# Silu and Softplus written out with Tanh, Exp and Ln in a Mamba-and-experts kernel on one core

## The reference, cut to what matters

```python
xz = xn @ W_in
xb, z = jnp.split(xz, 2, axis=-1)
xp = jnp.pad(xb, ((0, 0), (1, 1), (0, 0)))
xb = conv_w[:, 0] * xp[:, :-2] + conv_w[:, 1] * xp[:, 1:-1] + conv_w[:, 2] * xp[:, 2:] + conv_b
xb = jax.nn.silu(xb)
dt = jax.nn.softplus(xb @ W_dt + b_dt)
...
A_bar = jnp.exp(dt_t[:, :, None] * A)
h = A_bar * h + (dt_t * x_t)[:, :, None] * B_t[:, None, :]
y_t = jnp.einsum('bdn,bn->bd', h, C_t)
...
y = (y + D_param * xb) * jax.nn.silu(z)
```

## Time and profile before

| | |
|---|---|
| median of 3 runs | 2744.53 us (2736.11 to 2752.65) |
| profiled execution: time, span | 2752.65 us, 2750.8 us |
| instructions in the trace | 28773 |
| GpSimd busy | 2234.3 us, 81% |
| longest group: `drive`, L1175 | 512 of 2658 ns |
| scans, L702 | 512 of 2292 ns |
| decays, L1004 | 1024 of 682 ns |
| Softplus, L895 | 64 of 687 ns |
| Silu, L885 and L921 | 64 of 626 ns and 64 of 595 ns |

### The profile page before, as it was taken

One profiled execution on the slowest core, in us unless ns is written; L12 is line 12 of the kernel. 1 busy time (PEld: TensorE's weight loads), 2 busy tenths in 40 slices (PEclk: granted clock), 3 DMA queues, 4 the chain that ended last, 5 costly groups with the idle time before them and its releaser, 6 DMA issues.

```text
span 2750.8 us, 28773 instructions
## 1 busy us (share of the span) xinstructions
PE 2373.8 (86%) x9004; PEld 1696.4 (62%) x9004; DVE 2319.5 (84%) x2255; ACT 1621.4 (59%) x2892; POOL 2234.3 (81%) x1563
## 2 busy tenths in 40 slices
PE   3544798998989899998989999898989989898899
PEld 1222566676756666675666667666666766666678
DVE  1679898989989898988989899898989989898922
ACT  3465756557475656647576665757666575765311
POOL 1678888888989888888888899898888889887922
PEclk7677899999999899999999999999999999999999
DMA  4789898998989899898989999898999989898921
GB/s 114 201 194 253 200 239 216 241 229 219 253 211 246 219 231 237 217 241 211 240 219 240 237 222 250 205 252 220 252 223 221 247 198 244 216 253 214 242 60 51
DMA packets 338380, 596.80 MB, mean 217 GB/s; under 512 B 49697, under 2 KB 160289, under 8 KB 338225
## 3 DMA queue, kind: packets, MB, share of 16 engines
q0 software_dynamic: 72960, 243.30, 46.3%
q1 hardware_dynamic: 265264, 351.64, 40.5%
HBM read 349.89 MB, written 10.06 MB: 131 GB/s over the span
## 4 chain that ended last, share of the span: by engine, by line
PE 48%; POOL 16%; ACT 10%; DVE 10%; issue 9%; DMA 6%; SPq 0%; POOLq 0%; DVEq 0%; ACTq 0%
PE wbank L498 15%; PE mbank L510 9%; POOL unit L1175 7%; PE wbank L397 6%; DVE hbank L702 5%; DMA gsum<-unit 5%; PE wbank L440 4%; PE wbank L526 3%; PE wbank L385 3%; POOL act L1142 2%; POOL gsum L1187 2%; PE wbank L460 2%; DVE unit L716 2%; PE wbank L523 2%; ACT z L823 2%
## 5 line engine op out<-in xcount | busy, mean ns | idle before, releaser
L1175 POOL TENSOR_TENSOR unit<-dtx,b_bc 128x1024 f32<-128x1024 f32 x512 | 1355.3, 2658 | 5.5 <-DMA b_bc<-bc_scratch 3.1
L702 DVE TENSOR_TENSOR_SCAN hbank<-hbank,unit 128x1024 f32<-128x1024 f32 x512 | 1173.5, 2292 | 150.4 <-ACT hbank L1004 126.1
L1004 ACT ACTIVATE hbank<-dt,a_neg 128x512 f32<-128x512 f32 x1024 | 669.2, 682 | 279.8 <-DVE unit L716 246.2
L510 PE MATMUL mbank<-down_t,act 128*128 128x256 f32 x2048 | 526.4, 397 | 77.8 <-POOL act L1142 61.1
L716 DVE TENSOR_TENSOR unit<-hbank,c_bc 128x1024 f32<-128x1024 f32 x448 | 546.5, 1220 | 26.6 <-DVE hbank L702 1.0
L1142 POOL TENSOR_TENSOR act<-act,w_all 128x512 f32<-128x512 f32 x256 | 366.1, 1430 | 211.7 <-DVE act L680 196.4
L1187 POOL DMA_DIRECT2D gsum<-unit x448 | 451.5, 1008 | 100.3 <-DMA gsum<-unit 54.6
L498 PE MATMUL wbank<-h_t,up_t 128*128 128x256 f32 x2048 | 497.5, 387 | 22.8 <-DVE act L673 22.8
L510 PEld LDWEIGHTS mbank<-down_t,act 128*128 128x128 f32 x2048 | 399.7, 199 | 173.3 <-POOL act L1142 83.8
L498 PE MATMUL wbank<-h_t,gate_t 128*128 128x256 f32 x2048 | 487.9, 381 | 12.1 <-ACT gz L921 12.1
L498 PEld LDWEIGHTS wbank<-h_t,up_t 128*128 128x128 f32 x2048 | 394.4, 194 | 114.6 <-DVE act L673 35.2
(11 more groups left out here) (113 smaller groups left out, 2287.4 us busy)
## 6 DMA issues: line engine op xcount, KB each, us to landing
gsum<-unit POOLq DMA_DIRECT2D x448, 512.0 KB, 7.5
c_bc<-bc_scratch SPq DMA_DIRECT2D x464, 256.0 KB, 5.7
b_bc<-bc_scratch SPq DMA_DIRECT2D x448, 256.0 KB, 6.3
w_all<-w_scratch SPq DMA_DIRECT2D x256, 256.0 KB, 4.8
ht<-in_L_attn_x_dram SPq DMA_DIRECT2D x16, 512.0 KB, 5.2
w_out<-in_L_attn_W_out_dram SPq DMA_DIRECT2D x16, 512.0 KB, 5.6
ht<-in_L_attn_x_dram POOLq DMA_DIRECT2D x16, 512.0 KB, 8.8
out_dram<-xt SPq DMA_DIRECT2D x16, 512.0 KB, 3.3
```

Of the source, the lines that this page charges most:

```text
L510: m = eng.matmul(mbank[:, u * H:(u + 1) * H], act[:, (n - 1) % MOE_RING, j, u * P:(u + 1) * P], down_t[:, e, :], start=(e == 0 and u == 0) ...
L702: eng.tensor_tensor_scan(h, h, unit[:, g % RING, :, :].rearrange("p a t -> p (a t)"), 0.0, ALU.mult, ALU.add).then_inc(scanned, 1)
L1004: eng.activation(hbank[g % HB][:, a, :], dt[:, 2 * q + a, :], ACT.Exp, scale=a_neg[:, 2 * q + a, n:n + 1]).then_inc(decayed, 1)
L1175: eng.tensor_tensor(unit[:, g % RING, :, :], dtx[:, 2 * q:2 * q + 2, :], b_bc[:, s:s + 1, :].to_broadcast([P, 2, T]), ALU.mult).then_inc(d ...
```

## The change

Silu and Softplus are no longer asked of ScalarE by name. Silu(x) becomes x/2 * (1 + tanh(x/2)): ScalarE writes Tanh and VectorE does the rest in one scalar_tensor_tensor. For xb the half is folded into conv_w and conv_b, and Tanh is written back into the tile's work bank. The halves for the gates are folded into `diag_d` and into the new `half_ident`, with which y is now summed. Softplus(x) becomes relu(x) + ln(1 + exp(-|x|)): four ACTIVATEs and a tensor_tensor on VectorE. The banks of conv, dt and gate tiles are all freed by VectorE's last operation. The tasks of `silu_inputs` and `gates` handle one tile after the other with two or three steps each.

```diff
@@ xb_ready
-            need.wait_ge(silu_act, DK * (row + 1))
+            t = work.at["conv", row, DK - 1]
+            need.wait_ge(t.free, t.after)
...
@@ PE: mix
-                        m = eng.matmul(t.bank[:, :], ident[:, :], gsum[:, (2 * p + k) % SUMS, a, :], start=False,
+                        m = eng.matmul(t.bank[:, :], half_ident[:, :], gsum[:, (2 * p + k) % SUMS, a, :], start=False,
...
@@ VectorE: silu_inputs, step_sizes, gates
-                    need.wait_ge(conv_v, n)
+                    need.wait_ge(conv_v, 2 * n - 1)
                     eng.scalar_tensor_tensor(out=cv[:, 0:T - 1], in0=t.bank[:, 1:T], scalar=conv_w[:, q, 2:3],
-                                             in1=cv[:, 0:T - 1], op0=ALU.mult, op1=ALU.add).then_inc(t.free, 1)
-                    yield
-                for _ in range(4):
+                                             in1=cv[:, 0:T - 1], op0=ALU.mult, op1=ALU.add).then_inc(conv_v, 1)
+                    yield
+                    yield
+                    need.wait_ge(silu_act, n)
+                    if row and not pair:
+                        y = work.at["y", row - 1, q]
+                        need.wait_ge(y.full, y.after)
+                    eng.scalar_tensor_tensor(out=xb[:, xb_at(row, q), :], in0=t.bank[:, :], scalar=1.0, in1=cv, op0=ALU.add,
+                                             op1=ALU.mult).then_inc(t.free, 1)
+                    yield
+
+            def step_sizes(row, q):
+                for m_ in (2 * q, 2 * q + 1):
+                    t = work.at["dt", row, m_]
+                    yield
+                    need.wait_ge(soft_act, 4 * (DK * row + m_ + 1))
+                    eng.tensor_tensor(dt[:, m_, :], dt[:, m_, :], t.bank[:, :], ALU.add).then_inc(t.free, 1)
+                    yield
+                    yield
+
+            def gates(row):
+                for q in range(DK):
+                    t = work.at["gate", row, q]
+                    need.wait_ge(gate_act, DK * row + q + 1)
+                    eng.scalar_tensor_tensor(out=gz[:, q, :], in0=gz[:, q, :], scalar=1.0, in1=t.bank[:, :],
+                                             op0=ALU.add, op1=ALU.mult).then_inc(t.free, 1)
+                    yield
                     yield
...
@@ VectorE: mix
-                    gate = work.at["gate", row, q]
-                    need.wait_ge(gate.free, gate.after)
...
@@ VectorE: at the start
+            eng.tensor_scalar(conv_w[:, :, :], conv_w[:, :, :], 0.5, None, ALU.mult).then_inc(scaled_w, 1)
+            eng.tensor_scalar(conv_b[:, :], conv_b[:, :], 0.5, None, ALU.mult).then_inc(scaled_w, 1)
...
-                eng.tensor_scalar(diag_d[:, m_, :], ident[:, :], d_par[:, m_:m_ + 1], None,
+                eng.tensor_scalar(diag_d[:, m_, :], ident[:, :], d_par[:, m_:m_ + 1], 0.5, ALU.mult,
                                   ALU.mult).then_inc(scaled_w, 1)
+            eng.tensor_scalar(half_ident[:, :], ident[:, :], 0.5, None, ALU.mult).then_inc(scaled_w, 1)
...
@@ ScalarE: silu_inputs, step_sizes, gates
                     if n > 2:
-                        need.wait_ge(silu_act, n - 2)
+                        before = work.at["conv", *divmod(n - 3, DK)]
+                        need.wait_ge(before.free, before.after)
...
-                yield
-                yield
-                for q in (2 * pair, 2 * pair + 1):
-                    t = work.at["conv", row, q]
-                    need.wait_ge(t.free, t.after)
...
-                    eng.activation(xb[:, xb_at(row, q), :], conv[:, q % 2, :], ACT.Silu).then_inc(silu_act, 1)
-                yield
-                yield
+                    yield
+                    need.wait_ge(conv_v, 2 * n)
+                    eng.activation(t.bank[:, :], cv, ACT.Tanh).then_inc(silu_act, 1)
+                    yield
...
-                    eng.activation(dt[:, m_, :], t.bank[:, :], ACT.Softplus, bias=b_dt[:, m_:m_ + 1]).then_inc(t.free, 1)
+                    x = t.bank[:, :]
+                    eng.activation(dt[:, m_, :], x, ACT.Relu, bias=b_dt[:, m_:m_ + 1]).then_inc(soft_act, 1)
+                    eng.activation(x, x, ACT.Abs, bias=b_dt[:, m_:m_ + 1]).then_inc(soft_act, 1)
+                    need.wait_ge(soft_act, at + 2)
+                    eng.activation(x, x, ACT.Exp, scale=-1.0).then_inc(soft_act, 1)
+                    need.wait_ge(soft_act, at + 3)
+                    eng.activation(x, x, ACT.Ln, bias=1.0).then_inc(soft_act, 1)
...
-                for pair in range(2):
-                    yield
-                    for q in (2 * pair, 2 * pair + 1):
...
-                        eng.activation(gz[:, q, :], t.bank[:, :], ACT.Silu).then_inc(t.free, 1)
-                    for _ in range(4):
-                        yield
+                for q in range(DK):
...
+                    eng.activation(gz[:, q, :], t.bank[:, :], ACT.Tanh, scale=0.5).then_inc(gate_act, 1)
+                    yield
+                    yield
```

More of the change, by code:

```diff
@@ L133, in build @@
         ident = sb("ident", [P, P])
+        half_ident = sb("half_ident", [P, P])
         conv_w = sb("conv_w", [P, DK, 3])
@@ L223, in build @@
             sem(n) for n in ("norm_a", "norm_p", "normed", "conv_act", "conv_v", "silu_act"))
-        dtx_made, dt_cut = sem("dtx_made"), sem("dt_cut")
-        bc_out, w_stored = sem("bc_out"), sem("w_stored")
+        soft_act, dtx_made, dt_cut = sem("soft_act"), sem("dtx_made"), sem("dt_cut")
+        gate_act, bc_made, bc_out, w_made, w_stored = (
+            sem(n) for n in ("gate_act", "bc_made", "bc_out", "w_made", "w_stored"))
         b_in, c_in = [sem(f"b{k}_in") for k in range(B_RING)], [sem(f"c{k}_in") for k in range(C_RING)]
@@ L423, in gates @@
                     m.then_inc(t.full, 1)
-                    if q % 2:
-                        yield
-                        yield
-                        yield
+                    yield
                     yield
@@ L544, in _ @@
             need.wait_ge(weights_in, 16 * N_LOADS)
-            need.wait_ge(scaled_w, 6)
+            need.wait_ge(scaled_w, 9)
             stage_of = {"turn_in": turn_in, "silu_first": lambda r: silu_inputs(r, 0),
@@ L774, in _ @@
             stage_of = {"silu_first": lambda r: silu_inputs(r, 0),
-                        "silu_last": lambda r: silu_inputs(r, 1),
+                        "silu_last": lambda r: silu_inputs(r, 1), "gates": gates,
+                        "step_sizes0": lambda r: step_sizes(r, 0), "step_sizes1": lambda r: step_sizes(r, 1),
                         "mix0": lambda r: mix(r, 0), "mix1": lambda r: mix(r, 1),
@@ L876, in silu_inputs @@
                     yield
-                yield
-                yield
-                for q in (2 * pair, 2 * pair + 1):
-                    t = work.at["conv", row, q]
-                    need.wait_ge(t.free, t.after)
-                    if row and not pair:
-                        y = work.at["y", row - 1, q]
-                        need.wait_ge(y.full, y.after)
-                    eng.activation(xb[:, xb_at(row, q), :], conv[:, q % 2, :], ACT.Silu).then_inc(silu_act, 1)
-                yield
-                yield
+                    yield
+                    need.wait_ge(conv_v, 2 * n)
+                    eng.activation(t.bank[:, :], cv, ACT.Tanh).then_inc(silu_act, 1)
+                    yield
             def step_sizes(row, q):
                 for m_ in (2 * q, 2 * q + 1):
-                    t = work.at["dt", row, m_]
+                    t, at = work.at["dt", row, m_], 4 * (DK * row + m_)
                     need.wait_ge(t.full, t.after)
@@ L912, in gates @@
             def gates(row):
-                for pair in range(2):
-                    yield
-                    for q in (2 * pair, 2 * pair + 1):
[L916 to L920, removed]
-                        eng.activation(gz[:, q, :], t.bank[:, :], ACT.Silu).then_inc(t.free, 1)
-                    for _ in range(4):
-                        yield
+                for q in range(DK):
+                    t = work.at["gate", row, q]
+                    need.wait_ge(t.full, t.after)
+                    if row:
+                        p = work.at["proj", row - 1, 1]
+                        need.wait_ge(p.full, p.after)
+                    eng.activation(gz[:, q, :], t.bank[:, :], ACT.Tanh, scale=0.5).then_inc(gate_act, 1)
+                    yield
+                    yield
             def project(row):
```

## The result

The changed kernel takes 2782.5 us (2777.73 to 2789.72, 4 runs) against 2740.53 us (4 runs): ratio 1.0144, 95% interval 1.0115 to 1.0173. Slower was right, its size was not: +90 us forecast, +42 measured.

What follows compares the result with a forecast made beforehand. VectorE was taken to set the pace where nobody delays it. 16 x (3.3 - 1.7) for step_sizes1 and gates, 15 x (2.2 + 1.8) for step_sizes0 and conv, and 5 gave +90.6 on 2744.5: 2835 us, range 2745 to 2895.

Steps and rivals of the forecast that it cites:

- Sign: Whole kernel: the change makes it slower, given a chance of 0.82.
- loads: ScalarE's table loads: of 16 per batch row 8 go (10.3 us) and 8 stay, four of them at Ln.
- chain: Step sizes: Relu, Abs, Exp, load and Ln take 3.85 us from data to result, 3.16 more than Softplus.
- start: First batch row: nothing to hide behind, one exposed Softplus chain and some hand-overs cost 5 us once.
- step_sizes1: Second Softplus pair of a row: longer chains delay the scans, +3.3 us per row, bounds 1.2 and 6.3.
- step_sizes0: First Softplus pair, for the next row: VectorE full, nothing absorbed, +2.2 us per row, bounds 1.2 and 6.3.
- Gates: Gates' Silu: 2.4 us of added VectorE work less 4.1 of waits that go, -1.7 us per row.
- Conv: Conv tiles' Silu: added VectorE work and a Tanh wait, less idle time behind loads, +1.8 us per row.
- (a): Rival: load traffic idles VectorE and the Ln chains hide, so faster, 2690 us; chance 0.12.
- (b): Rival: PE waits for work banks now freed by VectorE, 2946 us, or 2890 at half of it; chance 0.11.
- (c): Rival: chains hide and only added VectorE work counts, 1.9 us per row plus 5, 2780 us; chance 0.09.
- (d): Rival: Exp and Ln share a table set, so step_sizes1's load back leaves the path, 2814 us; chance 0.06.

Runs made afterwards that it cites:

- soft_last: The kernel before with Softplus written out only for the second pair of a row (step_sizes1); median 2757.6 us, 0.49% slower.
- pe_twice_last: The kernel before with PE's product for the first dt tile of step_sizes1 made twice; 3.3 us more in units 0 to 3.
- soft_no_loads: Kernel before with only Softplus written out, but Tanh in place of Ln, so no table loads at the step sizes; 2750.0 us.
- adds_only: The kernel before, Softplus kept, with one tensor_tensor per dt tile added on VectorE, which also frees the bank; ratio 1.0024.
- soft_first: The kernel before with Softplus written out only for the first pair (step_sizes0); 0.48% slower.
- gates_only: The kernel before with only the gates' Silu written out as Tanh and VectorE operations; 2726.7 us, ratio 0.9945.
- silu_no_adds: The kernel before with both Silus replaced by a bare Tanh, without VectorE's last operation (results differ); 0.6% gained.
- conv_only: The kernel before with only the conv tiles' Silu written out; 0.84% slower.
- softplus_only: The kernel before with only Softplus written out, four ACTIVATEs and an add on VectorE; 2777.7 us, ratio 1.0137.

## Why the prediction was right and wrong

**Sign, loads, chain, start: right.** 8 loads per row stay, at Ln; the chain is 3.75 us; VectorE's row is 150.3. The start cost 6.7 us (first scan at 89.4 and 96.1) for 5.

**step_sizes1, the term that failed: +3.3 us per row forecast, about +0.3 measured by the stages** (+2.0 in units 0 to 3, -1.7 in units 4 to 10). By whole times soft_last, which has this part alone, is 0.49% or 13 us slower, 0.8 us per row, so the term was at least four times too large. Two steps of it were wrong. First, it took the data's arrival from one row. Windows around the start of that row, before and after (columns as in the earlier trace rows):

```profile
1184.00:1188.00 4.00, 2.17 (x11) 1.56 (x9) 3.90 (x4) 1.82 (x3) 3.73 (x3) 1.00 1.03 287
1188.00:1192.00 4.00, 3.21 (x6) 2.15 (x7) 3.90 (x4) 2.58 (x3) 3.94 (x3) 0.57 1.10 239
1192.00:1196.00 4.00, 4.00 (x14) 2.35 (x13) 3.90 (x4) 1.14 (x2) 3.43 (x3) 1.00 1.05 276
```

```profile
1198.00:1202.00 4.00, 2.89 (x14) 2.23 (x13) 3.90 (x4) 1.82 (x3) 3.67 (x3) 1.00 1.06 276
1202.00:1206.00 4.00, 4.00 (x12) 2.12 (x12) 3.90 (x3) 1.30 (x2) 3.25 (x2) 1.00 1.09 258
```

From 1188 to 1192 PE was granted 0.57 of its clock, part of the time 1.2 instead of 2.4 GHz, after a window in which it was busy 2.17 of 4 us. The rows of GpSimd and PE there, then PE's at the same place of an undisturbed row of the same trace (scan of unit 0 at 1509.45), then PE's in the changed kernel:

```profile
1184.27 0.87 POOL L1187 DMA_DIRECT2D gsum<-unit  x1 [1.36 <-DMA gsum<-unit]
...
1187.20 1.54 POOL L1142 TENSOR_TENSOR act<-act,w_all 128x512 f32<-128x512 f32 x1
...
1188.79 2.07 PE L510 MATMUL mbank<-down_t,act 128*128 128x256 f32 x4 [2.62 <-POOL act L1142]
1190.66 4.14 PE L397 MATMUL wbank<-xb,w_dt 128*128 128x512 f32 x8
```

```profile
1507.66 1.13 PE L510 MATMUL mbank<-down_t,act 128*128 128x256 f32 x4 [1.21 <-POOL act L1142]
1508.63 3.60 PE L397 MATMUL wbank<-xb,w_dt 128*128 128x512 f32 x8
```

```profile
1201.73 1.13 PE L510 MATMUL mbank<-down_t,act 128*128 128x256 f32 x4 [1.11 <-POOL act L1166]
1202.70 3.60 PE L400 MATMUL wbank<-xb,w_dt 128*128 128x512 f32 x8
```

The first w_dt product started 1.5 us after the scan of unit 0 there (1189.16), 0.8 us before it in the undisturbed row and 0.9 before it in the changed kernel (1203.61). Units 0 to 3 of the disturbed row took 21.35 us; of 13 rows of the same trace eight took 18.5 to 19.1 and five 20.8 to 21.5; in the second trace one is above 19.5. All five have a granted clock of 0.50 to 0.52 for 3.4 us from just before the scan of unit 0, and the other eight don't. But the clock is only half of it. GpSimd's `add` had waited 1.36 us for a DMA, its `act` for the experts came late, and PE waited 2.62 us for it instead of 1.21: 1.4 us. At the lower clock the four L510 then took 2.07 instead of 1.13 us and the product 4.14 instead of 3.60: 1.5 us. The late row of the second trace has the wait (2.98 us) and the full clock. I had read a disturbed row as the pattern.

Second, the sum pushed the scans by the chain's length and asked only for idle time in the same units. Medians per unit, us, the kernel before over its eight undisturbed rows, the others over 13:

```
unit              0     1     2     3     4     5     6     7     8
before         4.13  4.13  4.09  6.18  4.74  4.92  4.63  4.52  4.72
changed        4.13  6.11  5.71  4.74  4.51  4.92  3.54  4.51  4.34
pe_twice_last  4.13  6.89  5.04  6.18  4.74  4.92  4.63  4.52  4.72
```

Units 1 and 2 lose 3.6 us, near the 4.0 by which the chain was said to move the scans. What the sum missed is what comes back: 1.4 in unit 3, where waits of VectorE for tanh (0.7) and for decays (0.6) are gone, and 1.7 in units 4 to 8; it had let 0.7 be absorbed. A delay on ScalarE's side comes back later, a delay on PE's side does not. In the kernel before, units 6 and 8 wait for decays that stand in ScalarE's queue behind the projection's result, as here:

```profile
1223.28 0.39 ACT L935 ACTIVATE xt<-wbank 128x256 f32<-128x256 f32 x1 [3.68 <-PE wbank L442]
...
1224.80 2.30 DVE L702 TENSOR_TENSOR_SCAN hbank<-hbank,unit 128x1024 f32<-128x1024 f32 x1 [1.01 <-ACT hbank L1004]
```

With the scans later and PE not, that result is there in time: its first ACTIVATE (L935) starts 3.1 us after the scan of unit 6 in the kernel before and in pe_twice_last, and 1.6 us after it in the changed kernel, where the wait of 1.01 us is gone. That this is why is argued from these waits; shown is that all four kernels with Ln in the second pair have 30.1 in units 4 to 10, and that soft_no_loads (the same chain without the loads), adds_only and pe_twice_last have 31.8.

**step_sizes0: +2.2 forecast, +1.5 measured**, VectorE's adds 1.08 and the loads 0.44 of it. The two delays came as summed, +0.6 in unit 25 (3.92 to 4.51) and +1.5 in unit 26 (4.92 to 6.45, with L697's wait of 0.83 above); what failed is that nothing would be absorbed: unit 28 gave 0.6 back (5.12 to 4.51). By whole times it is less still: soft_first is 0.48% or 13 us slower, of which some 5 are at the start (first scan at 94.3), about 0.5 us per row.

**Gates: -1.7 forecast, -1.1 measured in gates_only**, by other terms: without the added work the gain is 1.0 instead of 4.1, and the 2.4 us of added work cost 0. Two wrong terms nearly cancelled, which is luck. The scans' rows of the whole traces, the kernel before and gates_only, show where the added work went:

```profile
L702 DVE TENSOR_TENSOR_SCAN hbank<-hbank,unit 128x1024 f32<-128x1024 f32 x512 | 1173.5, 2292 | 150.4 <-ACT hbank L1004 126.1
```

```profile
L710 DVE TENSOR_TENSOR_SCAN hbank<-hbank,unit 128x1024 f32<-128x1024 f32 x512 | 1173.3, 2292 | 103.7 <-ACT hbank L1009 79.2
```

The wait for decays fell by 46.9 us, 2.9 per row, and in silu_no_adds, with no work to put in its place, only to 100.0. So the added operations stand where VectorE would otherwise still have waited. **Conv: +1.8 forecast, +1.2 measured**: loads 0.3 for 1.2, added work 1.6 for 3.0. With the stages' terms the prediction's own sum gives 16 x (0.3 - 1.1) + 15 x (1.5 + 1.2) + 6.7 = 34 us, against 42 measured and 91 forecast.

**Rivals.** (a) is refuted by silu_no_adds: even without the added work only 0.6% is gained; and VectorE's idle time per row is 160.8 - 150.3 = 10.5 us, not below 9.3. (b), PE waiting for banks freed by VectorE, came in part. PE's rows of the changed kernel for the gates' and conv tiles' products, whose idle time in the kernel before was 0.6 and 7.6 us:

```profile
L424 PE MATMUL wbank<-xn_t,w_in 128*128 128x512 f32 x256 | 142.5, 685 | 28.2 <-DVE gz L608 20.7
...
L388 PE MATMUL wbank<-xn_t,w_in 128*128 128x512 f32 x256 | 124.3, 610 | 25.0 <-DVE xb L591 23.1
```

At the gates it is no cost that shows: gates_only has 28.0 us of it and is faster than the kernel before. In units 0 to 3 adds_only, which frees the dt banks from VectorE, is no slower. At the conv tiles (25.7 us in conv_only) no run separates it from the added operations. (c), 1.9 us per row with the chains hidden, came nearest in size, 2780 us, but not in mechanism, since the chains cost 2.4 + 0.4 us and 1.7 returned. (d) did not come: the loads back are there (49 before L1028). The Trainium skill (ScalarE: Activation LUTs, section Table sets: the hidden batching unit) names a set that holds both Exp and Ln; here 64 loads stand at Ln and 64 at an Exp or Tanh behind, so this program did not get it.

## What to carry to other kernels

Count table loads, but price each by what waits behind it: here the removal of Silu's 8 per row gained 0.6% (silu_no_adds), and 8 per row in and behind the Softplus chains cost 1.0% (softplus_only against soft_no_loads). Read a periodic kernel by stages over all its periods before taking durations from one. Before adding the length of a delayed chain, find the next waits in the same and the other engines' queues that the delay would fill.

## What was not expected of the hardware

The granted TensorE clock fell to its lower level for short times even in a kernel whose PE is busy 86%: for 3.4 us in the row above, after a window with 2.17 busy of 4 us, and for 10 us in the changed kernel (0.50 from 1254.2 to 1264.2). The row above cost 1.5 us by the clock and 1.4 by the wait for GpSimd: 21.35 us in units 0 to 3 where undisturbed rows take 18.5. The changed kernel's took 20.7 to 21.8 in all 13 rows, none at the lower clock there.
